# A transformer block with 16 small heads: a new layout of the software-pipelined step

## The reference

```python
xn = layernorm(x)
q, k, v = (split_heads(xn @ w.T * s + b))            # 16 heads of 8
attn = softmax(q @ k.T / sqrt(8))                     # 256 x 256 per head
a = (attn @ v merged) @ w_o.T * s_o + b_o
h = relu(s0 * (concat(xn, -xn) @ sign(k0))) * 2       # 128 -> 512
h = relu(s1 * (h @ sign(k1))) * 2                     # 512 -> 512
f = s2 * (h @ sign(k2))                               # 512 -> 128
out = x + a + f
```

## Time and profile before

| what | us |
|---|---|
| median of 3 runs | 333.4 (333.23 to 333.51) |
| the profiled execution | 330.62 |
| its span (first to last instruction) | 328.8 |
| TensorE busy | 291.4 (89%) |
| its weight loads | 181.4 (55%) |
| VectorE busy | 251.9 (77%) |
| ScalarE busy | 223.1 (68%) |
| GpSimd busy | 118.4 (36%) |
| chain that ended last, share of TensorE | 77% |

### The profile page before, as it was taken

The page is one execution under the profiler, slowest core; times in us unless marked ns, Lnnn a source line. Parts: engine busy times, 40 slices in busy tenths (PEclk is TensorE's granted clock), DMA queues, the critical chain, the costliest instruction groups (busy, mean ns, idle before and its releaser), DMA issues.

```text
span 328.8 us, 8642 instructions
## 1 busy us (share of the span) xinstructions
PE 291.4 (89%) x3252; PEld 181.4 (55%) x3252; DVE 251.9 (77%) x388; ACT 223.1 (68%) x339; POOL 118.4 (36%) x253
## 2 busy tenths in 40 slices
PE   6296899999999999999999999999999999989762
PEld 6184555565655656565656556565656565554321
DVE  4727886888878897978888788979788887787622
ACT  3204285878686777868786877777687868675780
POOL 3323343534433343535344333334353444211100
PEclk9679999999999999999999999999999999997997
DMA  4221213021312222121212122121222130210000
GB/s 115 65 72 32 83 26 92 20 84 50 86 34 68 67 54 79 32 73 54 82 50 85 37 79 56 53 80 40 63 53 80 52 85 22 64 52 3 17 19 16
DMA packets 24772, 18.69 MB, mean 57 GB/s; under 512 B 4668, under 2 KB 22556, under 8 KB 24732
## 3 DMA queue, kind: packets, MB, share of 16 engines
q1 hardware_dynamic: 24732, 18.15, 19.7%
HBM read 11.28 MB, written 6.29 MB: 53 GB/s over the span
## 4 chain that ended last, share of the span: by engine, by line
PE 77%; ACT 9%; issue 6%; DVE 6%; POOL 1%; POOLq 0%; ACTq 0%; DVEq 0%
PE ctx_bank L842 20%; PE work L865 19%; PE st_pair L817 10%; PE s_pair L831 7%; PE work L894 5%; PE work L872 5%; PE work L858 4%; ACT probs L511 3%; PE work L946 3%; PE st_pair L879 2%; PE work L933 2%; ACT xT L569 2%; DVE neg_max L622 2%; ACT xT_hi L569 1%; ACT qk L520 1%
## 5 line engine op out<-in xcount | busy, mean ns | idle before, releaser
L622 DVE TENSOR_REDUCE neg_max<-s_pair 128x4 f32<-128x1024 f32 x124 | 150.7, 1215 | 39.6 <-PE s_pair L831 37.7
L511 ACT ACTIVATE probs<-st_pair,exp_scale 128x1024 f32<-128x1024 f32 x124 | 138.4, 1116 | 41.6 <-PE st_pair L817 41.5
L842 PE MATMUL ctx_bank<-probs,v_ext 128*32 128x256 f32 x1024 | 69.5, 388 | 6.9 <-issue 3.8
L865 PE MATMUL work<-r_hi,w 128*128 128x256 f16 x256 | 60.4, 276 | 3.8 <-DVE w L761 2.1
L500 ACT ACTIVATE r_hi<-work 128x512 f16<-128x512 f32 x64 | 36.5, 593 | 35.5 <-PE work L865 29.5
L865 PE MATMUL work<-r_lo,w 128*128 128x256 f16 x256 | 60.0, 275 | 0.0
L817 PE MATMUL st_pair<-q_rows,k_rows 34*128 34x256 f16 x496 | 48.8, 275 | 8.2 <-ACT probs L511 7.4
L463 POOL TENSOR_SCALAR max_down<-neg_max 128x16 f32<-128x16 f32 x32 | 8.2, 256 | 128.5 <-DVE neg_max L622 128.5
L596 DVE SCALAR_TENSOR_TENSOR r_lo<-work,r_hi 128x512 f16<-128x512 f32 x64 | 42.3, 680 | 7.6 <-ACT r_hi L500 7.6
L831 PE MATMUL s_pair<-k_rows,q_rows 34*128 34x256 f16 x496 | 47.9, 271 | 0.2 <-DVE neg_max L622 0.2
L842 PEld LDWEIGHTS ctx_bank<-probs,v_ext 128*32 128x32 f32 x1024 | 29.3, 109 | 31.7 <-issue 18.9
(11 more groups left out here) (100 smaller groups left out, 353.4 us busy)
## 6 DMA issues: line engine op xcount, KB each, us to landing
k_rows<-k_scratch SPq DMA_DIRECT2D x64, 64.0 KB
q_rows<-q_scratch SPq DMA_DIRECT2D x32, 128.0 KB
xin<-x SPq DMA_DIRECT2D x16, 128.0 KB, 2.2
k_scratch<-qk_part SPq DMA_DIRECT2D x32, 64.0 KB, 2.1
q_scratch<-qk_part SPq DMA_DIRECT2D x32, 64.0 KB, 2.1
out<-outs SPq DMA_DIRECT2D x16, 128.0 KB, 1.9
q_rows<-max_rows SPq DMA_DIRECT2D x64, 4.0 KB
q_rows<-zeros SPq DMA_DIRECT2D x32, 8.0 KB
```

What stands on the lines that cost most here:

```text
L511: nc.scalar.activation(probs[j // 2 % 2][:, j % 2 * 2:j % 2 * 2 + 2, :, :].rearrange("p h k q -> p (h k q)"), pairs[j % len(pairs)][:, :], ...
L622: nc.vector.tensor_reduce(out=neg_max[:, j // QUARTER, :, j % QUARTER, :], in_=pairs[j % len(pairs)][:, :].rearrange("p (x q k) -> p x q k ...
L842: last = mm(ctx_bank[VC * j:VC * (j + 1), g % 2 * SEQ:(g % 2 + 1) * SEQ], v_ext[s.par(lag)][:, kt, GROUP * g + j, :], probs[g % 2][:, j, k ...
L865: last = mm(b[:, (m % 2) * SEQ:(m % 2 + 1) * SEQ], w1[:, kk, m * P:(m + 1) * P], part[:, kk, :], start=kk == n == 0, stop=kk == FB - 1 and ...
```

## The change

The step's layout is new on every engine; the work for a batch is the same. Slots on TensorE before and after (lag 0 unless told):

| slot | before | after |
|---|---|---|
| in each | exps' scores, maxima's scores | maxima's scores, exps' scores |
| 0 | q/k, max rows half 1 | layer 1 block 3 (lag 1), max rows half 1 |
| 1 | context 3 (lag 3), layer 0 | contexts 2 and 3 (lag 3) |
| 2 | context 0, layer 2 half | layer 0 half, layer 2 |
| 3 | layer 2 half, layer 1 block 0 | layer 0 half, v, transposes of lag -1 |
| 4 | context 1, max rows half 0, block 1 | contexts 0 and 1 |
| 5 | block 2, output product | max rows half 0, q/k of lag -1 |
| 6 | context 2, block 3 | output product, block 0 |
| 7 | v, transposes of lag -1 | blocks 1 and 2 |

`probs` has four buffers. The banks are shared anew (`WORK`). Steps run from -2 to 19. On SyncE the stores of q/k and the loads of rows stand in the step before the one that used to hold them, after the store of the half-0 maxima; the output is stored with lag 4. In the first batch ScalarE's queue stores q and loads the q rows, and ScalarE makes w1. The 30 warming transposes are replaced by 6 after the bound's product and 4 at the end of step 0. Cut to its core:

```diff
-        probs = [... for n in range(2)]
+        probs = [... for n in range(GROUPS)]
+        def max_pairs(b): return [st_pair, s_pair] if b == 0 else [s_pair]
+        def exp_pairs(b): return [st_pair, s_pair] if b == BATCH - 1 else [st_pair]
+        def load_q_rows(s, eng, lag):
+            s.wait(eng, hi_stored, 32, lag, 32)
+            s.wait(eng, lo_stored, 32, lag, 32)
+            for par in range(2):
+                eng.dma_start(q_rows[...], q_src...).then_inc(rows_loaded, 16)
 # SyncE, a step
+                has(-2): load xin;  has(1): store_max(s, 1, 0)
+                has(-1): wait rows_loaded of lag 0; store k (and q), high, then low part
+                has(1): store_max(s, 1, 1)
+                has(-1): zero_q_rows; load_k_rows high
+                has(4): store out
+                has(-1): load_q_rows (not in the first batch); load_k_rows low
 # GpSimd, a step
-                split_max 1, split_xT, y, residual, split_qk, ctxn, split_max 0, layer-norm
+                split_xT, split_max 1, split_qk, layer-norm, y, residual, ctxn, split_max 0
 # ScalarE, after exp j
-                0: qk  1: copy_max 1, relu_hi l0a, l0b  3: ffn  4: copy_max 0, ctxT
-                5: relu_hi l1a  6: relu_hi l1b  7: v, xT, xT_hi
+                0: relu_hi l1b, copy_max 1  2: relu_hi l0a, ffn  3: relu_hi l0b
+                4: xT, xT_hi, (first: load_q_rows), v, ctxT  5: copy_max 0
+                6: qk of lag -1, (first: w1, store_q)  7: relu_hi l1a
 # VectorE, after maximum j
-                0: relu_lo l1b, cast  1: turn 1, reciprocal  2: relu_lo l0a, l0b
-                3: ctx_back, stats  4: moments  5: turn 0  6: relu_lo l1a, outs
+                0: stats  1: relu_lo l1b, moments, turn 1  2: reciprocal  3: relu_lo l0a
+                4: ctx_back, relu_lo l0b  5: turn 0  6: outs  7: cast, relu_lo l1a
 # TensorE
-            def context(s, lag, g):
+            def context(s, lag, half):
+                s.wait(pe, probs_ready, HALF, lag, QUARTER * (half + 1))
+                s.wait(pe, ctx_turned, 2, lag, half)
+                for g in range(2 * half, 2 * half + 2):
+                    for kt in range(TT):
+                        for j in range(GROUP):
+                            last = mm(ctx_bank[...], v_ext[...], probs[g][:, j, kt, :], ...)
                 for j in range(HALF):
-                    if s.has(2):
-                        scores_for_exp(s, j)
                     if s.has(1):
                         scores_for_max(s, j)
+                    if s.has(2):
+                        scores_for_exp(s, 2, j)
-                    if s.first == 0 and j == 4:
-                        keep_warm(WARM_FIRST_STEP)
+                    if j == 3 and s.first == -1:
+                        ... most_psum ...; keep_warm(WARM_QK)
+                    if j == 7 and s.first == 0:
+                        keep_warm(WARM_ROWS)
```

More of the change, by code:

```diff
@@ new lines, in step @@
+                if s.has(1):
+                    s.wait(sp, max_rows_ready, 2, 1, 2)
+                    store_max(s, 1, 1)
+                if s.has(-1):
+                    if s.first != -1:
+                        zero_q_rows(s)
+                    load_k_rows(s, 0, hi_stored)
+                if s.has(4):
+                    s.wait(sp, out_ready, 1, 4, 1)
+                    sp.dma_start(out[s.batch(4):s.batch(4) + 1, :, :].rearrange("a (t p) c -> p (a t) c", p=P),
+                                 outs[s.par(4)][:, :, :]).then_inc(out_stored[s.par(4)], 16)
@@ L405, in step @@
             def step(s):
+                if s.has(0) and s.first != 0:
+                    split_xT(s, nc.gpsimd, pool, 0)
                 if s.has(2):
@@ new lines, in step @@
+                    if j == 3 and s.has(0):
+                        layer0(s, 1, take_bank(s, "l0b"))
+                    if j == 3 and s.has(1):
+                        b = take_bank(s, "v")
+                        for kt in range(TT):
+                            last = mm(b[:, kt * HID:(kt + 1) * HID], xT[s.par(1)][:, kt * P:(kt + 1) * P],
+                                      w_sb[:, 2, :], start=True, stop=True)
+                        last.then_inc(v_psum, 1)
+                    if j == 3 and s.has(-1):
+                        b = psum("xT") if s.has(1) else take_bank(s, "xT")
+                        s.wait(pe, xn_ready, 1, -1, 1)
+                        for tt in range(TT):
+                            c = (TT + tt) * P
+                            last = nc.tensor.transpose(b[:, c:c + P], xn[:, tt, :], ident[:, :])
+                        last.then_inc(xT_psum, 1)
@@ L924, in step @@
                         max_to_rows(s, 1, 0)
-                    if j == 4 and s.has(0):
-                        layer1_block(psum("l1a"), 1).then_inc(l1_psum, 1)
-                    if j == 5 and s.has(0):
-                        layer1_block(take_bank(s, "l1b"), 2)
-                    if j == 5 and s.has(3):
+                    if j == 5 and s.has(-1):
+                        b = take_bank(s, "qk")
+                        s.wait(pe, xT_copied, 2, -1, 2)
+                        for n in range(2):
+                            last = mm(b[:, n * SEQ:(n + 1) * SEQ], w_sb[:, n, :], xT[s.par(-1)][:, :],
+                                      start=True, stop=True)
+                        last.then_inc(qk_psum, 1)
```

481 lines of the change are left out of this document (236 added, 245 removed).

## The result

| | before | after |
|---|---|---|
| median of the timed runs | 333.31 us (332.99 to 333.51) | 311.02 us (310.78 to 312.61) |
| profiled execution, span | 330.62, 328.8 | 310.89, 309.0 |
| full step | 18.04 | 16.52 |
| TensorE busy | 89% | 91% |

The ratio is 0.934, 95% interval 0.931 to 0.937: 22.3 us less. The same kernel timed again gave 313.25 (see "The same kernels again"), so the 0.5 is less than two timings of it differ; the forecast's error is to be read from the full step.

The account below looks back on a forecast made before the run. It took TensorE's chain of waits as the bound, VectorE next. Full steps -11.4, start -3.2, step 1 -1.8, step 2 -1.7, end +2.3 sum to -15.8: 314.8 profiled, 317.6 us with 2.8 added; range 311.5 to 325.5.

Parts of the forecast that it names:

- the sum of the full step: Full step: waits and shape changes removed, VectorE delays added, giving 17.15 us, 0.88 less; -11.4 over thirteen steps.
- The four waits: TensorE's full step: two waits for the turned context bank (0.32, 0.14), one for an exp (0.44), one for xT (0.20) go.
- The shape changes: TensorE's full step: three contexts each lose 0.11 when a full-array group follows; merging them was counted as -0.30.
- VectorE, +0.23 +0.19 +0.10: Full step: late or long maxima on VectorE lengthen slots 0, 2 and 5 by these amounts in us.
- The start: Prologue up to step 1: step 1 begins at 22.4 instead of 25.59, -3.2 us, between 0 and -5.3.
- The end: Steps 16 on: late exps 5 to 7 and a last context of 32 matmuls cost +2.3 us, 0.9 to 4.0.
- From span to median: Timed median before lay 2.8 us above the profiled execution; the same difference was added to 314.8, giving 317.6.
- VectorE as the bound: Rival, full step: VectorE limits it to 17.65 us, -5.0 instead of -11.4, 324 us; chance 0.22 including "the swap does nothing".
- The late maxima rows: Rival: half-0 maxima rows stored in slot 5 land late and hold exp 0 of the next step; 342 us, chance 0.06.
- Better than counted: Rival, full step: VectorE's delays are absorbed, 16.8 us a step, 313 us; chance 0.07.
- The start gives nothing: Rival, prologue: with the clock at 0.50, step 1 still begins at 25.6; 320.8 us, chance 0.08.
- the swap does nothing: Rival, score order: only the layout counts, exps still wait 0.44 for fourteen steps, 6 us; chance within VectorE's 0.22.

Follow-up runs that it names:

- a_exp_first: The changed kernel with the exps' scores put back ahead of the maxima's scores in each slot: 310.29 us, ratio 0.929, full step 16.43.
- b_ctx_half: The kernel before with only contexts of two groups in slots 1 and 4 and four probs buffers: 350.91 us, ratio 1.053, full step 18.73.
- a_dve_late2: The changed kernel with a spare 0.33 us VectorE reciprocal between the turn and maximum 2: full step 16.88, 315.37 us in a single run.
- a_dve_extra: The changed kernel with a spare 0.33 us VectorE reciprocal behind maximum 2: 313.47 us, ratio 0.941, full step 16.52.
- a_ctx_split: The changed kernel with contexts one group at a time in slots 0, 1, 3 and 4: 326.74 us, ratio 0.977, full step 17.88.
- c_all_order: The changed kernel with exps' scores first, late memsets, no six warming transposes, warming transposes at the end and step 17's contexts later: 303.05 us, ratio 0.913.

## Why the prediction was wrong

**The step that failed is the sum of the full step**, 18.03 - 1.10 - 0.30 + 0.52 = 17.15. Measured: 18.04 - 1.10 - 0.56 + 0.16 = 16.54, against 16.52.
- The four waits, -1.10: all gone, as said. The reasons were partly wrong. The swap has no share in it (a_exp_first, 16.43). And the two waits of 0.32 and 0.14 were booked to the merging of contexts, which in the old layout costs 0.69 (b_ctx_half) where these terms gave a gain of 0.6 to 0.8. The filling of the slots decides, and the prediction has no term for it.
- The shape changes, -0.30: I counted three places at contexts. The groups that now stand beside others of their shape gained. By starts: layer 1 3.70 instead of 3.81, layer 2 1.03 instead of 1.15, v and transposes 0.76 instead of 0.86, layer 0 0.90 instead of 0.98, contexts 3.74 instead of 3.89: 0.56.
- VectorE, +0.23 +0.19 +0.10: measured 0.09, 0.00 and 0.07. The delays of the maxima were there, if smaller (maximum 2 starts 0.78 after its scores for 0.87, maximum 0 0.50 for 0.59), but I turned each into a delay of TensorE without asking when the next scores were due. In slot 2 that was 0.05 after the maximum's end. This was a near thing: a_dve_late2 shows that the next 0.33 is paid in full.

These two terms are 0.62 a step and 8.1 us over thirteen steps. By matmul busy time at most 0.81 a step was to be had, and 1.51 came. But the weight loads, busy for 10.77 of 18.03 before and 10.85 of 16.52 after, don't show either how full the step was; the starts did.

**The start**, -3.2, measured -0.8. The change also moves GpSimd's memsets beside VectorE's first layer-norm. The prediction does not name them, so it had them at nothing without a reason, and they held VectorE for 1.6 us; everything behind slid, and the first q/k product and 13 matmuls of layer 1, for 8 in the prediction, ran at half clock. Without the memset it is -3.9 (21.69). That the second queue would not be what ends last held.

**Steps 1 and 2**: 13.44 and 15.44 for 13.5 and 15.9.

**The end**, +2.3, measured +5.3, beyond its bound of 4.0. That the context stands ahead of exp 5's scores was seen; half clock was only the upper end, and it came with more than that. With the clock held it is +1.0.

**From span to median**, +2.8: it fell away, and should have been a width of the range, not a shift. That a measurement tells 0.2% from nothing was wrong for the same reason: after timed twice differs by 0.7%.

**Luck.** The start and the end came out 2.4 and 3.0 worse than forecast, and hid that much of the 8.7 by which the thirteen steps came out better. The time is 6.6 off; with the two right it would have been 12.

**The rivals.** VectorE as the bound (17.65 a step) is refuted by 16.52 and by a_dve_extra. The late maxima rows never showed: no exp 0 waited for a DMA. "Better than counted" (16.8 a step, 313) was the nearest; I gave it 0.07, since I read VectorE's 84% as a price and not as room. It was not priced as its own condition has it: with the three delays absorbed the prediction's bound is 16.63 a step, which gives 310.8 and lies below the range of 311.5 that was stated. "The start gives nothing" came nearly true in its term (-0.8), by the memset and not by the reason given. Of "the swap does nothing" the first half is shown and the second, that the exps go on waiting, is not so.

## What to carry to other kernels

When a step of a software pipeline has slots that each hold one long operation on another engine, give every slot at least as much matmul work as that operation's spacing, and even out the rest: here 0.7 to 1.4 us of 17 hung on it. A late operation costs only what its successor starts after the time at which it was due, so follow each delay to that time before adding it. Hold against each operation moved into the prologue what runs beside it there, and try filler matmuls in a thin end: here sixty cost less than the clock that they kept.

## What the hardware showed that was not expected

- VectorE's float32 tensor_scalar of 128x128, twice, took 2.20 us beside GpSimd's memset and 0.60 without.
- One and the same kernel has executions some microseconds apart (before: 329.8 to 335.4 in eight runs) by where the stretches at 1.2 GHz fall. The profiles show them in the first 51 us and the last 43, behind stretches in which TensorE had been idle for part of the time (kernel after, before 282.5: busy for 3.57 of the 5.00 us from 277.5). Full steps are free of them but for one: step 15 of a_ctx_split, 18.96 instead of 17.88.
- In c_all_order the records grant the full clock until 301 us, yet the eight matmuls of layer 0 and the first eight of layer 1 follow each other after 0.21 and not 0.11: the recorded clock can miss such a stretch, and the spacing shows it. In a_exp_first the records grant the full clock until 35.5 us, with the same 0.21 from 12 to 25 us.
